# Layer norms whose subtraction and scaling move from the vector engine to the scalar engine

## The reference

```
def _layernorm(x, axis=-1, eps=1e-05):
    m = jnp.mean(x, axis=axis, keepdims=True)
    v = jnp.var(x, axis=axis, keepdims=True)
    return (x - m) / jnp.sqrt(v + eps)
x = x + tanh(g_xattn[i]) * xattn_i(_layernorm(x), ctx)
x = x + tanh(g_ffn[i]) * ffn_i(_layernorm(x))          # i = 0..3
```

## Time and profile before

| what | value |
|---|---|
| timed runs | 2253.85, 2253.9 and 2258.35 us, median 2253.9 us |
| profiled execution | 2266.98 us, of which the span from first to last instruction is 2265.2 us |
| busy share of the span | PE 87%, DVE 86%, ACT 65%, POOL 42% |
| granted TensorE clock, mean | 0.955 of full speed |
| DMA | 55 MB in all, 24 GB/s |

### The profile page before, as it was taken

The page is one execution under the profiler, slowest core; times in us unless marked ns, Lnnn a source line. Parts: engine busy times, 40 slices in busy tenths (PEclk is TensorE's granted clock), DMA queues, the critical chain, the costliest instruction groups (busy, mean ns, idle before and its releaser), DMA issues. The chain is left out here.

```text
span 2265.2 us, 41466 instructions
## 1 busy us (share of the span) xinstructions
PE 1978.6 (87%) x12569; PEld 1576.8 (70%) x12569; DVE 1956.1 (86%) x7828; ACT 1472.5 (65%) x3637; POOL 949.1 (42%) x1374
## 2 busy tenths in 40 slices
PE   5877788888998899988998899998998899788677
PEld 4555567766886679766886579766886579667456
DVE  1289797998989999998989999998999999795982
ACT  3545467787677767787577767787577767477431
POOL 3232322555165534555165534555255543332441
PEclk9888898999999999999999999999999999898788
DMA  4000101001100101001100101001100001001000
GB/s 191 1 8 1 36 1 57 1 1 36 44 16 1 36 6 54 2 2 36 43 18 1 36 1 57 4 1 36 39 22 1 27 3 57 31 1 57 1 3 3
DMA packets 29503, 55.03 MB, mean 24 GB/s; under 512 B 2914, under 2 KB 10082, under 8 KB 28642
## 3 DMA queue, kind: packets, MB, share of 16 engines
q1 hardware_dynamic: 29282, 52.37, 7.1%
HBM read 51.31 MB, written 1.05 MB: 23 GB/s over the span
## 5 line engine op out<-in xcount | busy, mean ns | idle before, releaser
L265 DVE MATCH_REPLACE8 top_work<-top_eight,top_work 128x256 f32<-128x256 f32 x1664 | 667.9, 409 | 0.0
L267 DVE MAX8 top_eight<-top_work 128x8 f32<-128x256 f32 x1664 | 617.2, 412 | 0.0
L305 POOL TENSOR_TENSOR top_p<-top_p,top_rest 128x512 f32<-128x512 f32 x192 | 244.2, 1272 | 155.5 <-ACT top_rest L298 154.3
L851 PE MATMUL bank<-workP 128*128 128x256 f32 x1024 | 278.4, 396 | 22.7 <-ACT att_pP L991 10.7
L991 ACT ACTIVATE att_pP<-bank,att_tinyP 128x256 f32<-128x256 f32 x512 | 218.0, 487 | 60.4 <-DVE att_tinyP L1042 59.5
L851 PEld LDWEIGHTS bank<-workP 128*128 128x128 f32 x1024 | 180.1, 193 | 65.9 <-issue 24.2
L1042 DVE TENSOR_REDUCE att_tinyP<-bank 128x2 f32<-128x512 f32 x256 | 173.2, 680 | 22.4 <-PE bank L851 22.3
L273 POOL TENSOR_SCALAR top_nmax<-top_lead 128x2 f32<-128x2 f32 x192 | 37.2, 194 | 370.0 <-DVE top_lead L267 370.0
L645 PE MATMUL bank<-top_qk 128*128 128x256 f32 x512 | 150.0, 420 | 48.0 <-ACT top_p L286 40.7
L1013 POOL TENSOR_SCALAR workP<-workP,const 128x256 f32<-128x256 f32 x256 | 122.8, 486 | 152.8 <-PE bank L851 118.5
L298 ACT ACTIVATE top_rest<-top_work,top_nmax 128x256 f32<-128x256 f32 x384 | 173.9, 506 | 8.0 <-DVE top_work L265 7.6
(11 more groups left out here) (365 smaller groups left out, 4616.3 us busy)
## 6 DMA issues: line engine op xcount, KB each, us to landing
gelu_w<-in_pack3w SPq DMA_DIRECT2D x72, 256.0 KB, 3.0
top_qk<-in_pack3w SPq DMA_DIRECT2D x72, 256.0 KB, 2.8
pack<-in_pack SPq DMA_DIRECT2D x1, 4352.0 KB, 19.6
pack<-in_pack SPq DMA_DIRECT2D x1, 2266.0 KB, 9.7
pack<-in_pack SPq DMA_DIRECT2D x1, 1028.0 KB, 7.9
mix_wb<-in_ctx SPq DMA_DIRECT2D x1, 1024.0 KB, 4.8
x_in<-in_x SPq DMA_DIRECT2D x8, 128.0 KB, 2.1
ctx_tok<-in_ctx SPq DMA_DIRECT2D x8, 128.0 KB, 2.3
```

The costliest lines, as they stand in the source:

```text
L265: ins = nc.vector.match_replace(self.work[:, u % 2, j, :], eight, src, GONE)
L267: ins = nc.vector.max(eight, src)
L305: self.k.nc.gpsimd.tensor_tensor(v, v, self.rest[:, :, :], ALU.subtract).then_inc(*self.p_ready.one())
L851: mm = self.k.nc.tensor.matmul(self.banks[u % 2][:, j * T:(j + 1) * T], self.q1[:, u % self.RING, j * P:(j + 1) * P], self.kT, start=True, ...
```

## The change

DVE no longer writes y. ACT does, as Identity(scale * x + bias) with scale = `rstd` and bias = `shift`, both one column a token block, and `shift` = -mean * rstd is made by POOL. POOL has three instructions for a norm where it had one: -mean into `shift`, the power, and the product. DVE gets a wait ahead of BN_AGGR in the norms that follow a `start` stage (`before.shift_ready`), POOL one on `before.y_ready`, and ACT takes over the one on `before.turned`. The numbers of steps and parts are unchanged, so the strings of the outer blocks stay. `ORDER` is a new string of the same 543 letters (272 Q, 159 P, 112 M).

```diff
-    def dve_stats(self, dve):
+    def dve_stats(self, dve, before=None):
         ...
         self.chain.ready(dve)
+        if before is not None:
+            dve.wait_ge(*before.shift_ready.at(1))
         self.chain.mark(*(nc.vector.bn_aggr(self.mv[:, j, :], self.stats[:, j, :]) for j in range(NT)))
...
-    def dve_scale(self, dve, before=None):
+    def pool(self, pool, before=None):
+        pool.wait_ge(*self.var_ready.at(1))
         if before is not None:
-            dve.wait_ge(*before.turned.at(NT))
-        dve.wait_ge(*self.rstd_ready.at(1))
-        for j in range(NT):
-            self.k.nc.vector.tensor_scalar(self.y[:, j, :], self.x[:, j, :], self.mv[:, j, 0:1], self.rstd[:, j:j + 1],
-                                           ALU.subtract, ALU.mult).then_inc(*self.y_ready.one())
-
-    def pool(self, pool):
-        pool.wait_ge(*self.var_ready.at(1))
+            pool.wait_ge(*before.y_ready.at(NT))
+        self.k.nc.gpsimd.tensor_scalar(self.shift[:, :], self.mv[:, :, 0], -1.0, 1.0, ALU.mult, ALU.mult).then_inc(*self.less.one())
         self.k.nc.gpsimd.tensor_tensor(self.rstd[:, :], self.var[:, :], self.k.half[:, 0:NT],
                                        ALU.pow).then_inc(*self.rstd_ready.one())
+        pool.wait_ge(*self.less.at(1))
+        pool.wait_ge(*self.rstd_ready.at(1))
+        self.k.nc.gpsimd.tensor_tensor(self.shift[:, :], self.shift[:, :], self.rstd[:, :],
+                                       ALU.mult).then_inc(*self.shift_ready.one())
...
-    def act(self, act):
+    def act(self, act, before=None):
+        if before is not None:
+            act.wait_ge(*before.turned.at(NT))
+        act.wait_ge(*self.shift_ready.at(1))
+        for j in range(NT):
+            self.k.nc.scalar.activation(self.y[:, j, :], self.x[:, j, :], ACT.Identity, bias=self.shift[:, j:j + 1],
+                                        scale=self.rstd[:, j:j + 1]).then_inc(*self.y_ready.one())
         act.wait_ge(*self.turned.at(NT))
         self.k.nc.scalar.activation(self.yT[:, :], self.bank[:, 0:T], ACT.Copy).then_inc(*self.yT_ready.one())
```

More of the change, by code:

```diff
@@ L57 @@
 ORDER = (
[L58 to L63, removed]
+    "QQQPQPQQPQPQQMMQMPQMQQPPQQQPQQQMQQQQMPPPQQPMPPQQMPQQMPPPQQQQMPQQQQPQMPQQQQQPQMMQPQPQMMPQPQQQPQPMMQQPQQMPQMQPPQQQ"
+    "PMQQQQQMPQMPPQQQMMPQPMMPMQQMPPQQPMPQQQPPPPMPMQPMPPPPQQQMQPQQQMPQQPPPPPPPPMPQPQQMQQQMPQMPQQPQPQQQPQQPQPQPQQQQPQQQ"
+    "QPQQQQQMPQQMPQQQQMQPQQPQPQQQMQQQPQQQQMPQQPQPPQPQPQPQQQQQQQQPQMQQQPMPQPPQPQPMQQMQQQPMQMMPPPMQPQQMPMQMPQMPQPMPMQPM"
+    "MMPMQPMQPQQQQQMPMPQQMMPQMPMMMMPMMMMMMQMPQMPQMPQQQMPQMPQMQPMQPQQMPQMQQQQMPPMQQQPPMPQQMQQPQQMPQMQPQPPQPQQQMQPQQQQQ"
+    "QMPMMQQQPQQQPPQPMPPMMMPQPMQQQPQPMQPPMMQQQQQMMPMQPQQQQQQQPPQQQPQQQPPQQQQQQPMPPMQQQQQQMQPMQQMPQQQ")
+SKIPPED = {'Q': 304, 'P': 175, 'M': 121}
 ORDER_HEADS_2 = (
@@ L335, in __init__ @@
         self.var, self.rstd = k.sb(f"ln_var{side}", [P, NT]), k.sb(f"ln_rstd{side}", [P, NT])
+        self.shift = k.sb(f"ln_shift{side}", [P, NT])
         n = f"ln{side}{tag}_"
@@ L338, in __init__ @@
         self.var_ready, self.rstd_ready = k.sem(n + "var_ready", 1), k.sem(n + "rstd_ready", 1)
+        self.less, self.shift_ready = k.sem(n + "less", 1), k.sem(n + "shift", 1)
         self.y_ready, self.turned, self.yT_ready = k.sem(n + "y_ready", 2), k.sem(n + "turned", 2), k.sem(n + "yT_ready", 1)
     CUTS = 2
-    def dve_stats(self, dve):
+    def dve_stats(self, dve, before=None):
         nc = self.k.nc
@@ L463, in act @@
         if s == 1:
-            self.ln.act(act)
+            self.ln.act(act, self.start and self.start.ln)
             for half in range(2):
@@ L503, in pool @@
         if s == 0:
-            self.ln.pool(pool)
+            self.ln.pool(pool, self.start and self.start.ln)
             if self.load is not None:
@@ L526, in dve @@
                 dve.wait_ge(*self.load.at(3 * 16))
-            yield from self.ln.dve_stats(dve)
-        if s == 1:
-            self.ln.dve_scale(dve, self.start and self.start.ln)
+            yield from self.ln.dve_stats(dve, self.start and self.start.ln)
         if self.close(s) == 2:
@@ L613, in dve @@
             yield from self.ln.dve_stats(dve)
-        if s == 1:
-            self.ln.dve_scale(dve)
 class HeadsTop(TopSelect):
```

## The result

The changed kernel takes **2289.6 us** (median of 4 runs, 2287.0 to 2295.5) against 2256.1 us for the kernel before in the same job: a ratio of **1.0142, 95% interval 1.0123 to 1.0162**. It is slower by 32 us by the ratio (33 by the medians), where 24 us of gain were predicted, and outside the range of 2200 to 2265.

A forecast was written before the change was run, and what follows sets the result against it. DVE was taken to set the pace in the middle block outside the GELU stretch; 2.8 + 1.2 = 4.0 us a period, x 6 = 24 us, with 0 outside, gave 2230 us against 2253.9, range 2200 to 2265.

The forecast's parts named there:

- The pace of DVE: Middle block outside the GELU stretch: DVE is full, so removing y there gains its length, 2.8 us a period.
- The prices: Each norm: ACT y 0.49 us an instruction, POOL's negation 0.19 and product 0.25; 16 instructions a period on each engine.
- Norms of start3, start1, heads2 and GELU at 0: Middle block: three norms hang on a chain of about equal length, GELU's lies where PE is full; gain 0.
- Squares of mixed, 1.2 a period: Norm of mixed: more selection work covers DVE's 1.51 us wait for ACT's squares; gain 1.2 us a period, 0 to 1.5.
- ACT's 7.8 us a period as harmless: Middle block: ACT gets 16 instructions, 7.8 us a period, reaching 76% busy, far from the bound on the mean.
- POOL's 3.5 us as hidden: Middle block: POOL's 16 small instructions, 3.5 us a period, fit in its idle time; POOL at 49%.
- Outside the middle block at 0: One-lane norms lose 4 us by a longer chain, 12 norms in two-lane blocks gain 4 us; together 0.
- The rival that came true: Norms such as performer, gated, heads2: yT late for step 2 stops PE, all lanes' scores, then DVE; 2278 us, chance 0.17.
- Its turning point: Slower rival, middle block: the result turns when new stalls exceed 4.0 us a period, 0.5 us a norm.

The follow-up runs named there:

- the code alone: The changed code with the ORDER string of the kernel before: 2321.8 us, ratio 1.0296 against the kernel before.
- ACT's time: Kernel before, y on DVE, old order, with two extra ACT instructions of y's shape in step 1 of every norm, on which nothing waits: 2282.2 us, ratio 1.0092.
- POOL's chain: Kernel before, y on DVE, old order, but POOL makes shift and DVE's y waits for it, ACT untouched: 2293.2 us, ratio 1.0137.
- either half alone: Code of before under the new order with two neighbouring letters exchanged, 2317.5 us (1.0278); or the changed code under the old order, 2321.8 us (1.0296).

## Why the prediction was wrong, by its own steps

**The pace of DVE: the step that failed.** "DVE sets the pace, and only there is an instruction taken from DVE worth its own length", 8.3 us a period at most and 2.8 taken. In the middle block it is worth nothing that the runs can tell: with no y at all and the old order DVE is busy 35.8 us less and the six periods are 2.9 us longer; with the new order 3.0 shorter. A period lasts 256 us at its shortest with or without y. As I read it now, a slice in which DVE is full is full because its inputs were ready; how soon the next ones come is set by PE, ACT and POOL, whose order is written out as well. The earlier trace rows listed waits of 1 to 2 us and I read them as exceptions. They were the places where the rings close, and freed time flowed into them.

**The prices.** ACT y at 0.49 (0.48 to 0.49 measured), POOL's small ones at 0.19 and 0.25 (0.19 and 0.20 measured), 16 instructions a period: right. For the ACT price the Trainium skill's formula (*ScalarE: Activation LUTs*, What ACT_TABLE_LOAD costs, 479 ns as an estimate) agrees with the trace too.

**Norms of start3, start1, heads2 and GELU at 0: wrong.** Alone they cost 20.8 us over six periods on the old order (18 by the ratio). I had added the chain's own links and found them equal, 2.29 and 2.29. The sum left out what stands ahead of y in ACT's stream, which DVE's stream did not have.

**Squares of mixed, 1.2 a period: the wait went as forecast (1.5 to 0.3), the gain did not.** The order's cover did it, and the time reappeared at mix_rest and at POOL's sum.

**ACT's 7.8 us a period as harmless: wrong.** "ACT waited at the same place for PE's turn of DVE's y", and 76% on the mean, were the reasons. Two ACT instructions on which nobody waits cost 21 us by the ratio, 17.1 in the six periods. The lateness that I had named as a rival (ACT "is at 93% in slice 1062") is what happened.

**POOL's 3.5 us as hidden: wrong.** Two instructions of 0.2 us, alone, cost 0.47 us a norm on average on the old order. With y on ACT on the new order they cost nothing in the middle block and at most some 8 us elsewhere.

**Outside the middle block at 0: wrong.** The middle block alone is at 1.0090 and the whole change at 1.0142: 20 us and 12 us. In the traces the six periods begin at 373.4 to 383.4 us in six kernels with y on DVE in the outer blocks and at 385.7 to 390.1 in three with y on ACT there. I had +4 for the norms that run alone and -4 for the two lanes' blocks; which of the two failed was not told apart.

**The rival that came true** is the slower one, yT too late and the scores behind it, held at 0.17 and priced at 2278. Of its mechanism, ACT late at y with PE and then DVE behind it is seen at `gated`'s norm with the code alone and at `start1`'s after. Its place was wrong: PE stands one step earlier, at the turn (18.8 us in six periods against 8.1), and hardly for yT (0.5 in both). The wait at the performer's norm, which it named first, is there without any y. Its turning point, over 4.0 us of new stalls a period, was passed: the period grew by 2.6 us where 4.0 were to go, 6.6 in all. DVE's idle time grew by 48.3 us in six periods, 8.05 each, 5.5 of them being its relief. That its 2278 came within 12 us is in part luck: it put 24 us into the middle block, where 15 to 20 are, and nothing outside it. By the same page of the Trainium skill (Rules for kernel authors) adds and multiplications belong on VectorE. The result agrees, but the page's ground is the speed per element, and the runs put the loss at the place in the queue, at ACT's time and at the longer chain.

**How it adds up.** The code alone costs 66 us. Runs of one part each give 21 for ACT's time and 30 for POOL's chain (20 or more with y on ACT); y's place behind other lanes' work is seen in the timelines, but no run prices it alone. Some 10 to 16 us go through the granted clock, by the estimate above. These parts do not sum, as edits of very different size cost the middle block the same 3 to 4 us a period. That the new order wins back half is shown; which of its moved letters do it was not tried. No version that was tried with y off DVE beat the kernel before. The best of all is the one that computes no y, 0.7% faster, which bounds what another home for y could bring on these two orders; another order might hold more.

## What to carry to other kernels

Where all engines run orders written out together, a busy share says little of what relief is worth: take the work out altogether first, and if the kernel is no faster, no new home for it helps on that order. When work moves to another engine, price its place in that engine's queue (what stands ahead of it, and what stands behind its wait), not only its duration and its chain. And judge an order with the code it was laid out for: here either half alone costs 62 to 66 us, and both together 33.

## What the runs showed of the hardware

- GpSimd's tensor_scalar of 128x128 with two column operands takes 792 ns, beside 343 on VectorE and 489 on ScalarE, though the same engine takes 478 for 128x256 with one column operand (L718 after).
- With the code alone the granted clock fell to half right behind a slice in which PE was idle for half the time, in the middle of a block in which it is over 90% busy. In the kernel before the same pause, with the same 1.92 us busy in a slice of 4, left it at full. With filler turns of a constant in each norm the half-speed stretches fell from 79 to 34 us with the code alone and rose from 27 to 38 us in the kernel before.
- Periods of one trace are longer by 0.9 to 2.4 us where they hold 3.4 to 6.8 us more at half speed.
- A pair of ScalarE y instructions takes 0.87 to 0.89 us together, less than twice 0.49: 0.1 us overlaps.
